# A key stack zeroed by DMA from a row of zeros in DRAM, in place of a GpSimd memset

## The chip, the cores and the metric

The kernel runs on one core of a Trainium2 chip. The metric is the device time of one execution in microseconds (us); lower is better. Engines are named as in the profile: PE is TensorE's matrix multiply and PEld its weight load, DVE is VectorE, ACT is ScalarE, POOL is GpSimd, and SP is SyncE, the engine that issues every DMA of this kernel (its rows in a timeline say SPq).

## What is computed

A block of three stages on x of shape [4, 512, 128] in float32: half a mixture of experts, then an attention, then the same half mixture of experts again.

```python
x = x + 0.5 * ffn(layernorm(x), gate_w, Wg, Wu, Wd)     # 8 experts of 256, each takes its top 128 tokens
x = x + attn(layernorm(x), ...)                         # 16 heads of width 8
x = x + 0.5 * ffn(layernorm(x), gate_w, Wg, Wu, Wd)

def attn(x, Wa, ba, We, be, Wi, Wo, Wv, Wout, ...):
    aperture, expression = sigmoid(x @ Wa + ba), sigmoid(x @ We + be)
    inner, outer, v = x @ Wi, x @ Wo, x @ Wv            # each split in 16 heads of 8
    p = softmax(inner @ outer.T / sqrt(8))
    p = p * aperture[query] * expression[key]
    p = p / (p.sum(-1) + 1e-8)
    heads = rotate(p @ v)                               # a fixed rotation and scale for each head
    return heads @ Wout
```

## The kernel before

All five engines run programs that are written out by hand, with a semaphore for each hand-over; there is no scheduler. The order of the Python text is the order on each engine, and a wait holds everything that stands behind it on its engine.

**The stages.** The first mixture of experts runs until about 136 us of the span, the attention until about 390 us, the second mixture of experts to the end. The experts loop on PE is, for one expert, `gate_up` (12 matmuls, lines 1018 to 1020), `down` (L1035), `turn_down` (transposes, L1042) and `scatter` (L1050 and L1051, which add the expert's rows back to their tokens in four PSUM banks). DVE serves it with `gate_times_up` (L769), `weigh` (L777, L781, L783) and `make_place` (L761, four rows of 0 and 1 that say which token each slot goes to). After the last expert ACT scales the banks, PE turns them (L1079), and DVE adds them to x (`add_moe`, L801), normalizes (`norm_stats` L627 and L630, `norm_apply` L635 and L638), and PE projects (L1100, L1113).

**The key stack.** `k_stack` is [128, 4 groups, 4 heads, 512] in float32, 32 KB in each of 128 partitions, 4.19 MB in all. In the experts its two halves hold the gathered tokens (`picked_hi`, `picked_lo`), which `gate_up` reads. In the attention each half of 64 partitions holds 32 rows of keys for the heads of one parity and a row of ones below them (row 64 jj + 32); all other rows have to be zero, since the products run over all 128 partitions. So between the last `gate_up` of the first mixture of experts and the first load of keys the whole stack is zeroed, and the two rows of ones are written.

**Who clears and who waits.** POOL does it in `attention_constants` (lines 403 to 415), the last thing before it goes to sleep until the attention:

```python
pool.wait_ge(gate_up_done[0], 2 * MI * E)
nc.gpsimd.memset(k_stack[:].bitcast(F32), 0.0).then_inc(pool_consts, 1)
pool.wait_ge(pool_consts, 5)
nc.gpsimd.memset(v_ext[:, :, :, :, DH + 1:DH + 2], 1.0).then_inc(attention_consts, 1)
for jj in range(2):
    ...
    nc.gpsimd.memset(ones_rows.bitcast(F32), 1.0).then_inc(attention_consts, 1)
```

Two engines wait for `attention_consts` to reach 3, that is for the second row of ones: DVE at line 849, ahead of `add_bias(0)` (L835), and SP at line 339. What stands behind SP's wait, in this order: eight DMAs of `clear_max_rows` (L328, rows of zeros into the query stack); `store_parts(0)`, two stores of `part_hi` and two of `part_lo` (L314, 512 KB each, from 128 partitions); a wait for their landing; `load_stacks(0, 0)` (L323, four loads of 128 KB, each into 32 partitions of one half, two for the query stack and then two for the key stack); `store_parts(1)`; the loads of groups 1 to 3. The first products of the attention (`first_maxima`, L1133 on PE, reduced by L807 on DVE) wait for the first group's loads.

Of the kernel before, what the change touches and what calls it, by code (L numbers as in the profile page):

```python
# [12 lines left out]
F32 = mybir.dt.float32  # L13
# [34 lines left out]
def macaron_block(nc, x_in, Wa, ba, We, be, Wi, Wo, Wv, Wout, chi, beta_p, iv_p, ov_p, gate_w, Wg, Wu, Wd, out):  # L48
    B, S, D = x_in.shape
    H = Wa.shape[1]  # L50
    DH = D // H
    E, _, I = Wg.shape
    K = max(1, int(S / E * 2))
    C = S // P
# [3 lines left out]
    MI = I // P  # L58
    G = 4
    HG = H // G  # L60
# [5 lines left out]
    with ExitStack() as ctx:  # L66
        def sb(name, shape, dt=F32):
            return ctx.enter_context(nc.sbuf_tensor(name, shape, dt))

        def sem(name):  # L70
            return ctx.enter_context(nc.semaphore(name))
# [3 lines left out]
        zeros = sb("zeros", [P, S], F16)  # L75
# [68 lines left out]
        k_stack = sb("k_stack", [P, G, HG, S], F32R)  # L144
# [25 lines left out]
        row_i = sb("row_i", [P, 2], I32)  # L170

        parts_dram = nc.dram_tensor("parts_dram", [2, B, H, DH, 4, S], F32, kind="Internal").ap()
        zero_rows_dram = nc.dram_tensor("zero_rows_dram", [PAIRS, S], F32, kind="Internal").ap()

        ps = ctx.enter_context(nc.psum_tensor("ps", [P, 8, 512], F32))
# [3 lines left out]
        pool_consts = sem("pool_consts")  # L179
# [4 lines left out]
        gate_loaded = sem("gate_loaded")  # L184
        attn_weights_loaded = sem("attn_weights_loaded")
        zero_rows_stored = sem("zero_rows_stored")
        out_stored = sem("out_stored")

        def by(n, name):
            return [sem(f"{name}{i}") for i in range(n)]  # L190
# [17 lines left out]
        gate_up_done, silu_ready = by(2, "gate_up_done"), by(2, "silu_ready")  # L208
# [67 lines left out]
        def _(sp):  # L276
# [28 lines left out]
            sp.wait_ge(consts_made, 7)  # L305
            sp.dma_start(zero_rows_dram, zeros[0:PAIRS].bitcast(F32).rearrange("p (a t) -> p a t", a=1).broadcast_to([PAIRS, 2, S // 2])).then_inc(zero_rows_stored, 16)

            def store_parts(b):
                for half, (parts, ready, stored) in enumerate(((part_hi, qk_hi_ready, hi_stored), (part_lo, qk_lo_ready, lo_stored))):
                    for qk in range(2):  # L310
                        blocks = parts_dram[qk, b].rearrange("h d (m n) t -> m n (h d) t", m=2)
                        sp.wait_ge(ready, 2 * b + qk + 1)
                        twice = blocks[half] if qk == 0 else blocks[:, half]
                        sp.dma_start(twice.rearrange("n r t -> r n t"),  # L314
                                     parts[:, b % 2, qk, :].bitcast(F32).unsqueeze(1).broadcast_to([P, 2, S])).then_inc(stored[b % 2][qk], 16)
# [19 lines left out]
                                 max_rows[2 * jj:2 * jj + 2, g % 2, :].bitcast(F32)).then_inc(max_rows_loaded[g], 16)  # L335

            sp.wait_ge(scattered[0], B)
            sp.wait_ge(zero_rows_stored, 16)
            sp.wait_ge(attention_consts, 3)
            for g in range(G):  # L340
                clear_max_rows(g)
            store_parts(0)
            for qk in range(2):
                sp.wait_ge(hi_stored[0][qk], 16)
                sp.wait_ge(lo_stored[0][qk], 16)
            load_stacks(0, 0)
            store_parts(1)
            for g in range(1, G):
                load_stacks(0, g)
            load_max_rows(0, 0)  # L350
            store_parts(2)
            store_parts(3)

# [26 lines left out]
        def _(pool):  # L380
# [22 lines left out]
            def attention_constants():  # L403

                nc.gpsimd.memset(bias_row[:, 0:D], 0.0).then_inc(pool_consts, 1)
                nc.gpsimd.memset(v_ext[:], 0.0).then_inc(pool_consts, 1)
                pool.wait_ge(gate_up_done[0], 2 * MI * E)
                nc.gpsimd.memset(k_stack[:].bitcast(F32), 0.0).then_inc(pool_consts, 1)
                pool.wait_ge(pool_consts, 5)
                nc.gpsimd.memset(v_ext[:, :, :, :, DH + 1:DH + 2], 1.0).then_inc(attention_consts, 1)  # L410

                for jj in range(2):
                    pool.wait_ge(attention_consts, 1 + jj)
                    ones_rows = k_stack[64 * jj + 4 * DH:64 * jj + 4 * DH + 1].rearrange("r g (pp jj) t -> r g jj pp t", jj=2)[:, :, jj]
                    nc.gpsimd.memset(ones_rows.bitcast(F32), 1.0).then_inc(attention_consts, 1)
# [45 lines left out]
            affinity_parts(0)  # L461
            split_weights(0)
            attention_constants()
            pool.wait_ge(attention_consts, 3)
            pool.wait_ge(gates_ready, 2)
# [819 lines left out]
```

## Time and profile before

| | |
|---|---|
| time, median of 3 runs | 518.32 us (517.5 to 518.35) |
| span of the profiled execution, first to last instruction | 516.1 us, so 2.2 us less than the median |
| PE busy | 427.1 us (83%) |
| DVE busy | 400.4 us (78%) |
| ACT busy | 239.9 us (46%) |
| POOL busy | 68.6 us (13%) |
| moved by DMA | 26.03 MB, of it 25.74 MB on the one queue that SP feeds |

Only the span of the profiled execution is known beside the three times; the 2.2 us between it and the median lie before the first and behind the last instruction. A busy share is an average over the whole span. What one edit between two stages is worth is read from the stretch of the timeline around it.

### The profile page before, as it was taken

How to read it: one execution, taken by the hardware profiler on the slowest of the kernel's cores; microseconds unless marked ns; L12 is line 12 of the kernel's file. 1: busy time of each engine (PE TensorE's matmuls, PEld its weight loads, DVE VectorE, ACT ScalarE, POOL GpSimd, SP SyncE). 2: the span in 40 equal slices, each digit the busy share in tenths (PEclk: the TensorE clock that was granted, in tenths of full speed). 3: DMA queues.
4: the chain of work that ended last, by engine and by line, in shares of the span. 5: the costliest groups of instructions: out<-in, count | busy, mean ns of one | idle time of the engine just before them, and what ended most of it. 6: DMA issues, size and time to landing. Idle time of an engine off the chain costs nothing.

```text
span 516.1 us, 7820 instructions
## 1 busy us (share of the span) xinstructions
PE 427.1 (83%) x2252; PEld 250.8 (49%) x2252; DVE 400.4 (78%) x841; ACT 239.9 (46%) x439; POOL 68.6 (13%) x105
## 2 busy tenths in 40 slices
PE   2605999995588899999999999999996506999995
PEld 2501557773454445555555545554553402567773
DVE  6698848899689987778777777777655598768884
ACT  2400443330341267777676777766784201543332
POOL 5510002149000010000000000000002500001100
PEclk9999999998788799999999999999999655999999
DMA  5000012210058810111111111110110000012212
GB/s 166 1 0 1 1 30 62 61 31 0 4 213 276 297 61 25 37 37 43 42 42 42 42 42 42 42 42 1 35 31 0 0 0 2 1 33 59 61 32 81
DMA packets 24749, 26.03 MB, mean 50 GB/s; under 512 B 3634, under 2 KB 16438, under 8 KB 24726
## 3 DMA queue, kind: packets, MB, share of 16 engines
q1 hardware_dynamic: 24726, 25.74, 16.0%
q8 instruction: 12, 0.20, 0.2%
q14 instruction: 11, 0.09, 0.1%
HBM read 16.16 MB, written 9.44 MB: 50 GB/s over the span
## 4 chain that ended last, share of the span: by engine, by line
PE 69%; DVE 25%; issue 3%; ACT 2%; DMA 1%; DVEq 0%; ACTq 0%
PE ps L1133 12%; PE ps L1158 12%; PE ps L1148 10%; DVE neg_max L807 6%; PE ps L999 5%; PE ps L1035 5%; DVE heads_out L707 3%; PE ps L1018 3%; PE ps L1020 3%; PE ps L1019 3%; DVE values L704 3%; PE ps L1050 2%; PE ps L1051 2%; PE ps L960 2%; DVE probs L746 2%
## 5 line engine op out<-in xcount | busy, mean ns | idle before, releaser
L807 DVE TENSOR_REDUCE neg_max<-ps 128x1 f32<-128x512 f32 x256 | 163.4, 684 | 38.9 <-PE ps L1133 38.9
L597 ACT ACTIVATE probs<-ps 128x512 f32<-128x512 f32 x256 | 137.8, 598 | 64.6 <-PE ps L1148 62.9
L1133 PE MATMUL ps<-k_stack,q_stack 128*128 128x512 f32 x256 | 113.7, 452 | 4.8 <-DVE neg_max L807 3.5
L1148 PE MATMUL ps<-q_stack,k_stack 128*128 128x512 f32 x256 | 100.6, 403 | 0.2 <-ACT probs L597 0.2
L1133 PEld LDWEIGHTS ps<-k_stack,q_stack 128*128 128x128 f32 x256 | 49.0, 192 | 68.8 <-DVE neg_max L807 61.7
L1158 PE MATMUL ps<-probs,v_ext 128*32 128x512 f32 x512 | 68.2, 605 | 0.0
L1148 PEld LDWEIGHTS ps<-q_stack,k_stack 128*128 128x128 f32 x256 | 47.7, 190 | 12.7 <-ACT probs L597 5.7
L523 ACT CAST k_stack<-ps 128x512 fp32r<-128x512 f32 x32 | 17.2, 589 | 67.7 <-PE ps L999 67.7
L451 POOL TENSOR_TENSOR w_lo<-w_gu,w_hi 128x512 fp32r<-128x512 f32 x16 | 20.4, 1279 | 149.7 <-ACT w_hi L510 149.7
L769 DVE TENSOR_TENSOR vae_and_gates<-heads_out,ps 128x512 f32<-128x512 f32 x32 | 21.9, 687 | 19.7 <-ACT heads_out L531 17.7
L746 DVE TENSOR_TENSOR probs<-slot_row,slot 128x1024 f16<-128x1024 f16 x32 | 36.5, 1216 | 0.1
L1050 PE MATMUL ps<-q_stack,part_hi 128*128 128x512 f32 x64 | 28.5, 445 | 9.0 <-DVE part_hi L783 9.0
L761 DVE TENSOR_SCALAR q_stack<-token_row,indexT 128x512 fp32r<-128x512 f32 x64 | 33.9, 592 | 0.0
L476 POOL TENSOR_TENSOR v_ext<-vae_and_gates,expression 128x128 f32 (+1 forms) x16 | 6.5, 409 | 205.8 <-PE ps L1158 154.3
L999 PE MATMUL ps<-probs,xn_hi 128*128 128x512 f16 x64 | 26.8, 419 | 7.1 <-DVE probs L746 6.7
L1035 PE MATMUL ps<-vae_and_gates,wd_sb 128*128 128x512 f32 x64 | 30.5, 598 | 0.8 <-DVE vae_and_gates L769 0.8
L1018 PE MATMUL ps<-k_stack,w_hi 128*128 (+1 forms) x64 | 30.3, 474 | 0.8 <-ACT k_stack L523 0.8
L535 ACT COPY down_out<-ps 128x512 f32<-128x512 f32 x16 | 9.4, 588 | 45.4 <-PE ps L1035 45.4
L974 PE MATMUL ps<-ident,threshold_row 32*128 32x32 f32 x2 | 0.6, 309 | 33.4 <-DVE threshold_row L716 33.4
L999 PE MATMUL ps<-probs,xn_lo 128*128 128x512 f16 x64 | 26.9, 420 | 0.0
L1051 PE MATMUL ps<-q_stack,part_hi 128*128 128x512 f32 x64 | 26.9, 420 | 0.0
L531 ACT ACTIVATE heads_out<-ps 128x512 f32<-128x512 f32 x32 | 19.2, 599 | 14.9 <-PE ps L1020 13.1
(151 smaller groups left out, 574.8 us busy)
## 6 DMA issues: line engine op xcount, KB each, us to landing
parts_dram<-part_hi SPq DMA_DIRECT2D x8, 512.0 KB, 3.6
parts_dram<-part_lo SPq DMA_DIRECT2D x8, 512.0 KB, 4.9
q_stack<-parts_dram SPq DMA_DIRECT2D x32, 128.0 KB
k_stack<-parts_dram SPq DMA_DIRECT2D x32, 128.0 KB
w_gu<-in_L_ffn_Wg_dram SPq DMA_DIRECT2D x16, 128.0 KB, 2.1
w_gu<-in_L_ffn_Wu_dram SPq DMA_DIRECT2D x16, 128.0 KB, 2.2
wd_sb<-in_L_ffn_Wd_dram SPq DMA_DIRECT2D x16, 128.0 KB, 2.2
x<-in_L_attn_x_dram SPq DMA_DIRECT2D x4, 256.0 KB, 3.8
```

The source lines that it names most:

```text
L597: nc.scalar.activation(probs[:, u // HG, u % HG, :], ps[:, RING + ring_bank(step, u), :], ACT.Exp, scale=SCORE_SCALE).then_inc(probs_ready, 1)
L746: nc.vector.tensor_tensor(pick[:, b, c], slot_row[:].unsqueeze(1).broadcast_to([P, E, K]), slot[:, c, b * E:(b + 1) * E].unsqueeze(2).broa ...
L761: nc.vector.tensor_scalar(place[:, u, b, :], token_row[:], indexT[:, b, bass.ds(2 * i + o, 1)], None, ALU.is_equal).then_inc(place_ready[l ...
L807: nc.vector.tensor_reduce(neg_max[:, g, qt, col:col + 1], ps[:, ring_bank(step, u), :], AX.X, ALU.max, negate=True).then_inc(max_taken, 1)
L999: last = nc.tensor.matmul(ps[:, pick_bank(n) + k, :], half[:, C * b + c, :], pick[:, b, c, 4 * hf:4 * hf + 4, :], start=(c == 0), stop=(c ...
L1018: nc.tensor.matmul(ps[:, bank, :], w_hi[:, u, k, cols], tokens_hi, start=True, stop=False)
L1035: last = nc.tensor.matmul(ps[:, 6, :], wd_sb[:, u, m, :], hidden[:, u, m, :], start=(m == 0), stop=(m == MI - 1))
L1050: nc.tensor.matmul(ps[:, b, :], wy_hi[:, u, b, :], place[:, u, b, :], start=False, stop=False, skip_group_check=True)
L1051: last = nc.tensor.matmul(ps[:, b, :], wy_lo[:, u, b, :], place[:, u, b, :], start=False, stop=final, skip_group_check=True)
L1133: nc.tensor.matmul(ps[:, ring_bank(step, u), :], q_stack[:, g, pp, chunk(qt)], k_stack[:, g, 2 * pp + jj, :], start=True, stop=True).then_ ...
L1148: nc.tensor.matmul(ps[:, RING + ring_bank(step, u), :], k_stack[:, g, j, chunk(c)], q_stack[:, g, j // 2, :], start=True, stop=True).then_ ...
L1158: last = nc.tensor.matmul(ps[32 * j:32 * j + 32, 6, :], v_ext[:, g, c, j, :], probs[:, c, j, :], start=(c == 0), stop=(c == C - 1))
```

## The change

The memset of the stack on POOL goes. In its place SP writes a row of zeros of 32 KB into DRAM (from the fp16 tile `zeros`, one DMA), waits for it and for the last `gate_up`, and then issues two DMAs of 2.1 MB: each reads that one row 64 times and writes it into one half of 64 partitions of `k_stack`. POOL waits for both before it writes the rows of ones. The two memsets of the rows of ones stay, and so do both waits for `attention_consts`.

```diff
+        zero_stack_dram = nc.dram_tensor("zero_stack_dram", [1, G * HG * S], F32, kind="Internal").ap()
...
+        k_stack_cleared = sem("k_stack_cleared")
...
             sp.dma_start(zero_rows_dram, zeros[0:PAIRS]...).then_inc(zero_rows_stored, 16)
 
+            sp.dma_start(zero_stack_dram.rearrange("a (p t) -> (a p) t", t=S // 2), zeros[0:2 * G * HG].bitcast(F32)).then_inc(zero_rows_stored, 16)
+            sp.wait_ge(zero_rows_stored, 32)
+            sp.wait_ge(gate_up_done[0], 2 * MI * E)
+            for jj in range(2):
+                sp.dma_start(k_stack[64 * jj:64 * jj + 64].bitcast(F32).rearrange("r g j t -> r (g j t)"),
+                             zero_stack_dram.broadcast_to([64, G * HG * S])).then_inc(k_stack_cleared, 16)
...
             sp.wait_ge(scattered[0], B)
-            sp.wait_ge(zero_rows_stored, 16)
             sp.wait_ge(attention_consts, 3)
...
                 nc.gpsimd.memset(v_ext[:], 0.0).then_inc(pool_consts, 1)
-                pool.wait_ge(gate_up_done[0], 2 * MI * E)
-                nc.gpsimd.memset(k_stack[:].bitcast(F32), 0.0).then_inc(pool_consts, 1)
-                pool.wait_ge(pool_consts, 5)
+                pool.wait_ge(pool_consts, 4)
                 nc.gpsimd.memset(v_ext[:, :, :, :, DH + 1:DH + 2], 1.0).then_inc(attention_consts, 1)
 
+                pool.wait_ge(k_stack_cleared, 32)
                 for jj in range(2):
```

On SP, between the last weights of the first experts and the attention's first stores, the kernel before has these rows (what is written, what is read, the shape):

```order
L306 DMA zero_rows_dram<-zeros 4x1x256 [waits consts_made]
L328 DMA q_stack<-zero_rows_dram 1x1024 [waits attention_consts,zero_rows_stored,scattered0]
L328 DMA q_stack<-zero_rows_dram 1x1024 x7
L314 DMA parts_dram<-part_hi 128x2x512 [waits qk_hi_ready]
```

The changed kernel has these at the same place:

```order
L308 DMA zero_rows_dram<-zeros 4x1x256 [waits consts_made]
L310 DMA zero_stack_dram<-zeros 32x256
L314 DMA k_stack<-zero_stack_dram 64x8192 [waits gate_up_done0,zero_rows_stored]
L314 DMA k_stack<-zero_stack_dram 64x8192
L337 DMA q_stack<-zero_rows_dram 1x1024 [waits attention_consts,scattered0]
L337 DMA q_stack<-zero_rows_dram 1x1024 x7
L323 DMA parts_dram<-part_hi 128x2x512 [waits qk_hi_ready]
```

Three DMAs came in ahead of `clear_max_rows`, and nothing else moved on SP. On POOL, behind the last expert's weights, the kernel before has:

```order
L405 MEMSET bias_row 128x128
L406 MEMSET v_ext 128x2048
L408 MEMSET k_stack 128x8192 [waits gate_up_done0]
L410 MEMSET v_ext 128x64 [waits pool_consts]
L415 MEMSET k_stack 1x8x512 [waits attention_consts] x2
```

The changed kernel has there:

```order
L413 MEMSET bias_row 128x128
L414 MEMSET v_ext 128x2048
L416 MEMSET v_ext 128x64 [waits pool_consts]
L422 MEMSET k_stack 1x8x512 [waits attention_consts,k_stack_cleared]
L422 MEMSET k_stack 1x8x512 [waits attention_consts]
```

One memset left, and the first row of ones took on a wait for the two DMAs. The order on the other engines is the same.

## Rows read from the trace of the kernel before

**Rows 1.** The page: busy time of two engines, and the last chain by engine.

```profile
PE 427.1 (83%) x2252; PEld 250.8 (49%) x2252; DVE 400.4 (78%) x841; ACT 239.9 (46%) x439; POOL 68.6 (13%) x105
PE 69%; DVE 25%; issue 3%; ACT 2%; DMA 1%; DVEq 0%; ACTq 0%
```

**Rows 2.** Timeline of POOL: start us, us, engine, line, operation, count, idle before.

```profile
114.69 6.93 POOL L408 MEMSET k_stack<- 128x8192 f32 x1 [2.00 <-PE ps L1020]
121.68 0.37 POOL L410 MEMSET v_ext<- 128x64 f32 x1
122.10 7.24 POOL L415 MEMSET k_stack<- 1x4096 f32 x2
```

**Rows 3.** Timeline of DVE in the same stretch.

```profile
116.02 5.88 DVE L781 CAST part_hi<-weighted 128x512 fp32r<-128x512 f32 x1
121.94 0.69 DVE L783 TENSOR_TENSOR part_hi<-weighted,part_hi 128x512 fp32r<-128x512 f32 x1
122.54 7.86 DVE L761 TENSOR_SCALAR q_stack<-token_row,indexT 128x512 fp32r<-128x512 f32 x4
...
131.04 0.43 DVE L781 CAST part_hi<-weighted 128x512 fp32r<-128x512 f32 x1
```

**Rows 4.** Timeline of PE, the end of the first mixture of experts.

```profile
116.76 1.88 PE L1035 MATMUL ps<-vae_and_gates,wd_sb 128*128 128x512 f32 x4
...
132.34 0.77 PE L1050 MATMUL ps<-q_stack,part_hi 128*128 128x512 f32 x1 [5.95 <-DVE part_hi L783]
...
135.89 2.14 PE L1079 MATMUL ps<-ident,combined 128*128 128x128 f32 x16
```

**Rows 5.** Timeline of PE, the end of the second mixture of experts.

```profile
502.13 1.88 PE L1035 MATMUL ps<-vae_and_gates,wd_sb 128*128 128x512 f32 x4
...
509.32 1.91 PE L1079 MATMUL ps<-ident,combined 128*128 128x128 f32 x16
```

**Rows 6.** Waits of SP: who was waited for, us, times, longest.

```profile
SPq L339 <- POOL k_stack L415: 21.8, 1, 21.8
```

**Rows 7.** Timeline of SP: DMA issues, start us and us.

```profile
136.13 2.31 SPq L328 DMA_DIRECT2D q_stack<-zero_rows_dram  x8
143.42 1.51 SPq L314 DMA_DIRECT2D parts_dram<-part_hi  x2
147.21 1.17 SPq L314 DMA_DIRECT2D parts_dram<-part_lo  x2
151.48 0.84 SPq L323 DMA_DIRECT2D q_stack<-parts_dram  x2
...
190.94 0.89 SPq L323 DMA_DIRECT2D q_stack<-parts_dram  x2
```

**Rows 8.** Windows, all engines; last two columns: DMA share and GB/s.

```profile
144.30:144.60 0.30, 0.00 (x0) 0.00 (x0) 0.27 (x4) 0.00 (x0) 0.00 (x0) 1.00 0.90 341
147.50:148.00 0.50, 0.50 (x4) 0.50 (x4) 0.50 (x3) 0.24 (x1) 0.00 (x0) 0.50 0.00 0
150.80:151.20 0.40, 0.40 (x2) 0.02 (x1) 0.40 (x2) 0.37 (x1) 0.00 (x0) 1.00 0.25 87
160.00:166.00 6.00, 4.86 (x9) 1.75 (x9) 6.00 (x11) 0.00 (x0) 0.00 (x0) 0.81 0.91 262
172.00:181.00 9.00, 7.70 (x25) 4.13 (x23) 8.93 (x16) 2.39 (x5) 0.11 (x1) 0.81 1.03 379
192.40:192.80 0.40, 0.40 (x2) 0.32 (x3) 0.00 (x0) 0.11 (x1) 0.00 (x0) 1.00 0.85 200
192.80:194.00 1.20, 1.20 (x9) 0.93 (x7) 0.91 (x2) 0.60 (x1) 0.00 (x0) 1.00 0.77 273
```

**Rows 9.** Timeline of DVE at the start of the attention.

```profile
139.47 1.11 DVE L638 TENSOR_SCALAR xn<-x,mean_var,rstd 128x128 f32<-128x128 f32 x4
...
150.58 0.88 DVE L835 TENSOR_TENSOR vae_and_gates<-ps,bias_row 128x320 f32<-128x320 f32 x2
...
156.75 9.65 DVE L807 TENSOR_REDUCE neg_max<-ps 128x1 f32<-128x512 f32 x16
```

## The prediction

> **What bounds the kernel now.** I read the page first: PE is busy 83% of the span, DVE 78%, and the chain that ended last is 69% PE and 25% DVE [rows 1]. POOL and DMA carry almost none of it. So an edit on POOL and on the DMA queue can only count through what they hold up, and that is read in the timeline of the 40 us in which the stack is cleared.
>
> POOL's timeline comes next. Its memset of the stack starts at 114.69, when the last `gate_up` is done, and takes 6.93 us; the two rows of ones end at 129.34, and with that `attention_consts` is complete [rows 2]. The reader is to see in DVE's timeline what this does beside it. The cast L781 takes 5.88 us from 116.02, until POOL's memset is over, and 0.43 us at 131.04, when POOL is idle; four L761 take 7.86 us beside the rows of ones [rows 3]. DVE stands still while POOL's memset runs. PE waits for it: the last scatter starts at 132.34 after 5.95 us of idle time, and the turning L1079 at 135.89, which is 19.1 us after the last `down` at 116.76 [rows 4]. The second mixture of experts runs the same instructions with no memset beside them, and there it is 7.2 us, from 502.13 to 509.32 [rows 5]. So the memsets cost the end of the first stage 11.9 us.
>
> What the constants are waited for comes last. They were ready at 129.34, SP's 21.8 us behind them [rows 6] ended there, and the next thing that SP needed, the last scatter, came at 136.13 [rows 7]. Before, the clear and its rows of ones were 6.8 us early for SP and, with L835 at 150.58, 21 us early for DVE [rows 9].
>
> **What the change does, part by part.**
>
> Removed: 6.93 us of memset on POOL, and with it the stall of L781. If nothing else bound, L1079 would start at 116.8 + 7.2 = 124.0 instead of 135.9, for the two rows of ones then no longer fall on L761. That is the prize, 11.9 us.
>
> Added, at no cost: the 32 KB row of zeros is written at about 107.6, behind L306, while SP has nothing to do until 114.7; POOL's 0.37 us memset of `v_ext` runs earlier.
>
> Added, with a price: the constants now come later. Step by step, with r for the rate of the two clears in GB/s and 4194 KB to write:
> - issue at 114.7, since SP waits for the same semaphore as POOL did [rows 2];
> - 0.9 us to the first data, as from the issue at 143.42 to 144.3 [rows 7, 8];
> - 4194/r;
> - 0.6 us from the last data, about 150.9, to the reader's release at 151.48 [rows 7, 8];
> - 7.3 us for the two rows of ones and their waits [rows 2].
>
> So the constants are ready at 123.5 + 4194/r. Behind that, on SP, which is the engine with most queued behind the wait: 2.3 us for the eight DMAs of `clear_max_rows`; then the four stores of `store_parts(0)`. Their data are long ready by then, for the first stage ended earlier. Before, they took from 143.42 to 151.48, 8.1 us, of which about 1.0 us was a gap (no data from 147.1 to 148.1, a wait for `part_lo`) [rows 7, 8]; without it 7.1 us. So the first loads are issued 9.4 us after the constants. They are ready 3.5 us later: in the attention's loop four like them are issued from 190.94 and their data end at 194.0, plus 0.6 us less 0.2 us for a slower issue there [rows 7, 8]. Another 0.5 us for the first product, and DVE starts L807 at 136.9 + 4194/r. Before it started at 156.75 [rows 9]. What lies behind is the same work in the same order, paced by DVE. The net is
>
> 4194/r − 19.9 us, with break-even at r = 211 GB/s.
>
> DVE's own wait at line 849 costs nothing beside this: L835 to L807 was 6.2 us before [rows 9], against 13.4 us on SP's path.
>
> **The rate** is what the trace does not show: nothing in it writes 64 partitions with 32 KB each, or reads one row of DRAM 64 times. The rows nearest to it are the loads of the stacks, each into 32 partitions of one half: 262 GB/s while 160 to 166 us hold nothing else, 273 and 200 GB/s in two pieces of the loop's loads. The stores from 128 partitions ran at 379 GB/s [rows 8]. So a narrower destination is slower here. By 379 the clears take 11.1 us, by 262 16.0 us, by 200 21.0 us. I take the middle of 200 and 262, about 230 GB/s: the small loads change the half every 128 or 256 KB, the clears stay for 2.1 MB in one, so I go below their mean, but not below their slowest piece. 4194/230 = 18.2 us: the last clear lands at 134.4, the constants are ready at 141.7, SP issues the first loads at 151.1 and DVE starts L807 at 155.1. The net is −1.6 us: 11.9 us of stall taken away, 10.3 us of them given back to a later clear. Against the span of 516.1 us that is 514.5 us, and with the 2.2 us around it 516.7 us, 1.6 us below the median of 518.32 us. Its own range, for 262 to 200 GB/s, is −3.9 to +1.1 us, 514.4 to 519.4 us.
>
> **A cap on the gain.** However fast the clear, the rows of ones move with it, and they stop DVE's L638 as they stopped L761. Without stalls L638 would first run at 139.47 − 11.9 = 127.6. At 379 GB/s the clear has landed at 127.3 and the rows of ones fill 127.3 to 134.6, so the first L638 group ends about 135 in place of 140.6. The gain is then 5.6 us, not the 8.8 us of the formula. At 300 GB/s (rows of ones from 130.2 to 137.5) the second group is caught, and the gain is about 5 us.
>
> **The rivals.**
>
> *Full rate.* The clears run at 300 to 379 GB/s, for the source is one 32 KB row and each piece is long. For it: the 128-partition stores, 379 GB/s [rows 8]. Against it: no load into a part of the partitions came near it. It gives −5.0 to −5.6 us by the cap, 512.7 to 513.3 us.
>
> *Half rate.* A transfer into one half of the partitions gets half of what the full width gets, 379/2 = 190 GB/s, and the second clear queues behind the first. 4194/190 = 22.1 us, so +2.2 us: 520.5 us. For it: the narrow loads are all below the wide stores. Against it: 262 GB/s over 6 us is 1.4 times 190, though those loads alternate between the halves. The Trainium skill (SBUF — State Buffer, Door 1: The DMA port swizzle) states this as a rule: partitions 0 to 63 reach 8 of 16 ports, 196 GB/s at 1 MiB and 218 in the limit, and two transfers on the two halves gain only 6%. By its 218 the sum would be 19.2 us and −0.6 us, by its 196 21.4 us and +1.5 us. No run here has shown it for a transfer of this size.
>
> *One hot row (slower).* All DMA engines read the same 32 KB of DRAM at the same time, and the rate falls below 190 GB/s because of it. Its place is the wait of POOL's first row of ones for the clears; it decides for slower from 200 GB/s down (+1.0 us), at 150 GB/s it is +8.1 us (526.4 us), at 170 +4.8 us. For it: no row shows such a read of any size. Against it: nothing. The Trainium skill (DMA: Bandwidth & Descriptors, Latency and other measured facts) has copies between HBM tensors with a large power of two between rows fall from 207 to 103 GB/s; by 103 the clears would take 40.7 us, and the sum would be +20.8 us. No row here bears on it.
>
> *No effect.* The DVE stall is not POOL's doing, and the clear is early anyway. The pair 5.88 and 0.43 us for one instruction [rows 3] speaks against it: 518.3 us.
>
> **How the numbers follow.** The forecast (200 to 262 GB/s) 0.45; full rate, with what lies between 262 and 300, 0.17; half rate 0.18; one hot row 0.17; no effect 0.03. About 0.2% (1.04 us) is what a measurement of this kernel can tell from no change: faster from 222 GB/s up, slower from 200 down. Of the forecast's 0.45, 0.28 lie above 222, 0.15 between and 0.02 at the slow end. Faster: 0.28 + 0.17 = 0.45. Same: 0.15 + 0.04 of half rate + 0.03 = 0.22. Slower: 0.02 + 0.14 + 0.17 = 0.33. The range reaches from the cap, 512.7 us, to 524.4 us, which is 162 GB/s: it leaves out what lies below 162 GB/s, somewhat over 0.1, and a few in a hundred below the cap.
>
> **What the changed profile would show.** L781 at about 116 takes 0.43 us, four L761 1.7 us, and L1079 starts near 124. Both clears are issued near 114.8; the DMA windows behind give the rate, and the first row of ones starts near 134.4. L638 between 134 and 142 is drawn out to the end of the rows of ones. SP's longest wait in this stretch is still for the rows of ones, now to about 141.7, and `clear_max_rows` follows at once. PE is idle for several us before the first L1133, near 154.6, where before it went from L1113 to L1133 without a pause. Behind that both traces run alike, shifted by one amount. Wrong would be: a rate outside 200 to 262 GB/s; stores or loads that take longer than 7.1 and 3.5 us once they are back to back; or a second clear that overlaps the first at full width.

## The result and the profile after

The changed kernel takes 524.52 us (median of 4 runs, 522.56 to 525.46) beside 518.34 us for the kernel before (4 runs). The ratio is 1.0115, with a 95% interval of 1.0091 to 1.0138: slower by some 6 us, where a gain of 1.6 us was forecast. The line numbers of the changed kernel are higher: L781 is now L788, L761 L768, L638 L645, L807 L814, L1035 L1042, L1079 L1086, L1100 L1107, L1133 L1140, L339 L347. In the runs further below they shift by a few lines again, and the view names the tiles.

The page after: busy times and the last chain by engine, which answer to [rows 1].

```profile
PE 431.8 (83%) x2252; PEld 254.3 (49%) x2252; DVE 395.4 (76%) x841; ACT 239.4 (46%) x439; POOL 61.7 (12%) x104
PE 74%; DVE 19%; issue 3%; ACT 2%; DMA 1%; DVEq 0%; ACTq 0%
```

POOL lost its 6.9 us and DVE 5 us of busy time, and the kernel is slower. The timelines show why. First those of DVE and of PE at the end of the first mixture of experts:

```profile
116.63 0.43 DVE L788 CAST part_hi<-weighted 128x512 fp32r<-128x512 f32 x1
...
117.70 1.67 DVE L768 TENSOR_SCALAR q_stack<-token_row,indexT 128x512 fp32r<-128x512 f32 x4
```

```profile
116.77 1.88 PE L1042 MATMUL ps<-vae_and_gates,wd_sb 128*128 128x512 f32 x4
...
123.97 1.91 PE L1086 MATMUL ps<-ident,combined 128*128 128x128 f32 x16
```

The cast that took 5.88 us takes 0.43 us, the four L761 that took 7.86 us take 1.67 us, and the turning starts at 123.97 in place of 135.89 [rows 3, 4]. So the prize of 11.9 us was there and was won. The timelines of SP and POOL, the time to landing of the two clears, and SP's wait show what came after it:

```profile
114.73 1.16 SPq L314 DMA_DIRECT2D k_stack<-zero_stack_dram  x2
144.63 2.26 SPq L337 DMA_DIRECT2D q_stack<-zero_rows_dram  x8
146.93 1.09 SPq L323 DMA_DIRECT2D parts_dram<-part_hi  x2
148.07 1.99 SPq L323 DMA_DIRECT2D parts_dram<-part_lo  x2
153.95 0.83 SPq L332 DMA_DIRECT2D q_stack<-parts_dram  x2
```

```profile
137.45 7.10 POOL L422 MEMSET k_stack<- 1x4096 f32 x2 [24.81 <-DMA k_stack<-zero_stack_dram]
```

```profile
DMA to landing us min/median/max: 12.2/17.2/22.1
```

```profile
SPq L347 <- POOL k_stack L422: 28.7, 1, 28.7
```

The first clear (issued at 114.7) lands 12.2 us later, at 126.9, the second (issued at 115.3) after 22.1 us, at 137.4. Between the two landings lie 10.5 us for 2097 KB, which is 200 GB/s. POOL starts the rows of ones at once, they end at 144.55, SP goes on at 144.63, and the first loads are issued at 153.95, where before it was 151.48 [rows 7]. The start of the attention on DVE and on PE:

```profile
138.32 6.38 DVE L645 TENSOR_SCALAR xn<-x,mean_var,rstd 128x128 f32<-128x128 f32 x4
...
158.70 1.89 DVE L814 TENSOR_REDUCE neg_max<-ps 128x1 f32<-128x512 f32 x3 [3.25 <-PE ps L1140]
163.40 7.87 DVE L814 TENSOR_REDUCE neg_max<-ps 128x1 f32<-128x512 f32 x13 [2.81 <-PE ps L1140]
```

```profile
157.90 1.62 PE L1140 MATMUL ps<-k_stack,q_stack 128*128 128x512 f32 x3 [5.69 <-issue]
159.32 1.91 PE L1107 MATMUL ps<-xnT,wi_sb 128*128 128x512 f32 x2
161.02 1.91 PE L1107 MATMUL ps<-xnT,wo_sb 128*128 128x512 f32 x2
161.94 8.38 PE L1140 MATMUL ps<-k_stack,q_stack 128*128 128x512 f32 x13
```

The reader is to see two pauses of DVE here. The first one, 3.25 us, is the wait for the first loads. The second one, 2.81 us, stands between the third and the fourth reduction: PE does the last query and key projection there (L1107), at 1.91 us for each pair of matmuls that takes 1.02 us at full clock (at 136.67 of the same trace). The granted clock was 0.50 from 157.9 to 163.0, the lower of the two levels, after PE had idled for 5.69 us. The kernel before has the same projection at the same place, at full clock:

```profile
155.51 0.97 PE L1133 MATMUL ps<-k_stack,q_stack 128*128 128x512 f32 x3
156.32 1.02 PE L1100 MATMUL ps<-xnT,wi_sb 128*128 128x512 f32 x2
157.18 1.02 PE L1100 MATMUL ps<-xnT,wo_sb 128*128 128x512 f32 x2
157.63 7.82 PE L1133 MATMUL ps<-k_stack,q_stack 128*128 128x512 f32 x13
```

There DVE started at 156.75 and ran 16 reductions without a pause [rows 9], so its fourth began at about 158.6. Now the fourth starts at 163.40, 4.8 us later.

### The profile page after: what moved, and what is told of

It is laid out like the page before. It is cut to its first block, busy times and chain, and to the rows that moved or that the text cites. A ratio compares the mean times of both kernels' runs of the same rounds, so it can differ in the third digit from the quotient of the medians.

```text
span 523.2 us, 7824 instructions
## 1 busy us (share of the span) xinstructions
PE 431.8 (83%) x2252; PEld 254.3 (49%) x2252; DVE 395.4 (76%) x841; ACT 239.4 (46%) x439; POOL 61.7 (12%) x104
## 4 chain that ended last, share of the span: by engine, by line
PE 74%; DVE 19%; issue 3%; ACT 2%; DMA 1%; DVEq 0%; ACTq 0%
PE ps L1140 13%; PE ps L1165 12%; PE ps L1155 10%; PE ps L1042 5%; PE ps L1006 5%; DVE neg_max L814 4%; PE ps L1025 3%; PE ps L1027 3%; PE ps L1026 3%; DVE heads_out L714 3%; DVE values L711 3%; PE ps L1057 3%; PE ps L1058 2%; PE ps L967 2%; PE ps L1107 2%
## 5 line engine op out<-in xcount | busy, mean ns | idle before, releaser
L814 DVE TENSOR_REDUCE neg_max<-ps 128x1 f32<-128x512 f32 x256 | 163.6, 685 | 44.9 <-PE ps L1140 44.9
L1140 PE MATMUL ps<-k_stack,q_stack 128*128 128x512 f32 x256 | 114.9, 461 | 10.8 <-issue 5.7
L1140 PEld LDWEIGHTS ps<-k_stack,q_stack 128*128 128x128 f32 x256 | 49.9, 196 | 75.4 <-DVE neg_max L814 61.5
L1042 PE MATMUL ps<-vae_and_gates,wd_sb 128*128 128x512 f32 x64 | 30.5, 598 | 0.8 <-DVE vae_and_gates L776 0.8
L1057 PE MATMUL ps<-q_stack,part_hi 128*128 128x512 f32 x64 | 26.5, 414 | 0.4 <-DVE part_hi L790 0.4
L768 DVE TENSOR_SCALAR q_stack<-token_row,indexT 128x512 fp32r<-128x512 f32 x64 | 26.7, 481 | 0.0
L1027 PE MATMUL ps<-k_stack,w_lo 128*128 (+1 forms) x64 | 25.2, 394 | 0.0
```

The costliest lines, as they stand in the source:

```text
L768: nc.vector.tensor_scalar(place[:, u, b, :], token_row[:], indexT[:, b, bass.ds(2 * i + o, 1)], None, ALU.is_equal).then_inc(place_ready[l ...
L814: nc.vector.tensor_reduce(neg_max[:, g, qt, col:col + 1], ps[:, ring_bank(step, u), :], AX.X, ALU.max, negate=True).then_inc(max_taken, 1)
L1027: nc.tensor.matmul(ps[:, bank, :], w_lo[:, u, k, cols], tokens_hi, start=False, stop=True).then_inc(gate_up_done[l], 1)
L1042: last = nc.tensor.matmul(ps[:, 6, :], wd_sb[:, u, m, :], hidden[:, u, m, :], start=(m == 0), stop=(m == MI - 1))
L1057: nc.tensor.matmul(ps[:, b, :], wy_hi[:, u, b, :], place[:, u, b, :], start=False, stop=False, skip_group_check=True)
L1140: nc.tensor.matmul(ps[:, ring_bank(step, u), :], q_stack[:, g, pp, chunk(qt)], k_stack[:, g, 2 * pp + jj, :], start=True, stop=True).then_ ...
```

## The experiments

Four runs ask what sets the rate of the clears, three what stands behind it. All were timed beside the kernel before on the same chip (its median was 518.94 us beside the first four and 518.01 us beside the last three); ratios are against it.

**One clear at full width, from one row.**

```diff
-            for jj in range(2):
-                sp.dma_start(k_stack[64 * jj:64 * jj + 64]...,
-                             zero_stack_dram.broadcast_to([64, G * HG * S])).then_inc(k_stack_cleared, 16)
+            sp.dma_start(k_stack[:]..., zero_stack_dram.broadcast_to([P, G * HG * S])).then_inc(k_stack_cleared, 16)
```

> The changed kernel, but the stack is cleared by one DMA into all 128 partitions, still from the one row of 32 KB in DRAM. Theory A (a transfer into 64 partitions gets half of the full width's rate): the clear runs at about 380 GB/s, lands about 12.5 us after its issue in place of 22.7 us, the rows of ones start near 127.5, and the time is near 513 us (the cap of about 5.5 us below before). Theory B (one hot row in DRAM sets the 200 GB/s): the clear still takes 21 us or more and the time stays near 524 us.

515.25 us, ratio 0.9911 (0.9874 to 0.9948). Time to landing of the clear, and the timelines of POOL and DVE:

```profile
DMA to landing us min/median/max: 12.0/12.0/12.0
```

```profile
127.11 7.10 POOL L421 MEMSET k_stack<- 1x4096 f32 x2 [13.42 <-DMA k_stack<-zero_stack_dram]
```

```profile
127.68 6.69 DVE L644 TENSOR_SCALAR xn<-x,mean_var,rstd 128x128 f32<-128x128 f32 x4
...
151.85 9.64 DVE L813 TENSOR_REDUCE neg_max<-ps 128x1 f32<-128x512 f32 x16
```

The same 4.19 MB from the same row land after 12.0 us, not 22.7 us after the first issue. Less the 1.5 us of latency that the prediction used (0.9 and 0.6 us), that is 10.5 us, 400 GB/s. One hot row is no limit even at twice the rate. The rows of ones now fall on the first group of normalizations (L638 before, L644 here), as the cap said, and DVE starts 4.9 us earlier than before.

**Two clears into the halves, from rows of their own.** The row of zeros becomes an image of 128 rows.

```diff
-        zero_stack_dram = nc.dram_tensor("zero_stack_dram", [1, G * HG * S], F32, kind="Internal").ap()
+        zero_stack_dram = nc.dram_tensor("zero_stack_dram", [P, G * HG * S], F32, kind="Internal").ap()
...
+            sp.dma_start(zero_stack_dram.rearrange("p (a t) -> p a t", t=S // 2),
+                         zeros[:].bitcast(F32).unsqueeze(1).broadcast_to([P, 2 * G * HG, S // 2])).then_inc(zero_rows_stored, 16)
...
-                             zero_stack_dram.broadcast_to([64, G * HG * S])).then_inc(k_stack_cleared, 16)
+                             zero_stack_dram[64 * jj:64 * jj + 64]).then_inc(k_stack_cleared, 16)
```

> The changed kernel, its two clears into 64 partitions each kept, but they read 128 rows of 32 KB of their own (4.19 MB of zeros, stored in DRAM from about 12 us on, far ahead). Theory A: nothing changes, the second clear lands 21 to 23 us after the first issue, 524 us. Theory B: the clears run at 300 to 380 GB/s and the time is near 513 us.

523.75 us, ratio 1.0085 (1.0057 to 1.0114). Time to landing:

```profile
DMA to landing us min/median/max: 12.8/17.7/22.5
```

With rows of their own the halves are no faster, so the hot row is ruled out from this side too.

**One clear at full width, from rows of its own.** The image, and the one DMA of the first run.

> Both at once: one DMA into 128 partitions, from 128 rows of its own. Theories A and B both expect about 380 GB/s and 513 us; if it is faster than the run with one row at full width, the hot row costs something at the higher rate. If it stays at 200 GB/s, both fall, and the size of the pieces (32 KB) is the next suspect.

513.21 us, ratio 0.9889 (0.9857 to 0.9920). Time to landing, and DVE:

```profile
DMA to landing us min/median/max: 12.3/12.3/12.3
```

```profile
151.85 9.65 DVE L816 TENSOR_REDUCE neg_max<-ps 128x1 f32<-128x512 f32 x16
```

The landing takes 12.3 us against 12.0, and the first reduction (L807 before) starts at 151.85 in both: whether the source is one row or 128 makes no difference here. The medians lie 2 us apart, but the intervals of the two ratios overlap.

**The halves in turn.** 16 DMAs of 256 KB, from one row, the half changed after each. POOL waits for all 16.

```diff
+            for piece in range(8):
+                at = slice(1024 * piece, 1024 * piece + 1024)
                 for jj in range(2):
-                    ...
+                    sp.dma_start(k_stack[64 * jj:64 * jj + 64]...[:, at],
+                                 zero_stack_dram[:, at].broadcast_to([64, 1024])).then_inc(k_stack_cleared, 16)
```

> The changed kernel with its two clears cut into 16 of 256 KB that go to the two halves in turn (4 KB in each of 64 partitions), from the same one row. The reason that the prediction gave for a rate between 200 and 262 GB/s was that small loads change the half and so overlap. If that holds, about 260 GB/s, the last clear lands about 17.5 us after the first issue, and the time is 518 to 520 us. If two halves in turn do not overlap, 200 GB/s and 524 us.

522.69 us, ratio 1.0071 (1.0047 to 1.0094). The issues, the time to landing, and POOL:

```profile
L316 SPq DMA_DIRECT2D k_stack<-zero_stack_dram x16: 513/597/602, 115.6 to 125.1; - x16
```

```profile
DMA to landing us min/median/max: 3.5/7.7/11.5
```

```profile
136.69 7.10 POOL L424 MEMSET k_stack<- 1x4096 f32 x2 [22.64 <-DMA k_stack<-zero_stack_dram]
```

From the first issue at 115.6 to POOL's start it is 21.1 us; less 1.5 us that is 19.6 us and 214 GB/s. Changing the half gives 7% over the two large clears, not the 30% that the reason for my rate needed. All pieces were issued by 125.7, some 11 us before POOL's start, so SP's issue is not what held them.

**The projection ahead of the first products.**

```diff
-            first_maxima(0, range(RING))
             project_qk(3)
+            first_maxima(0, range(RING))
```

> The changed kernel, but PE runs project_qk(3) before the first three products of first_maxima(0) in place of behind them, in the 5 us in which it waits for the first loads anyway. Theory: 2.8 us of the loss come from this projection, which a PE at half clock (1.91 us for each of its two products) puts between the third and the fourth product while VectorE has nothing else left. Then VectorE's 2.8 us of idle time behind its third reduction go, L814 runs through, and the time falls by 2.8 us, to near 521.7 us. Rival: the pause is the loads' or the throttle's own, and the time stays at 524.5 us.

520.21 us, ratio 1.0060 (1.0041 to 1.0080), against 1.0115 (1.0091 to 1.0138) without the edit; the intervals do not touch. Timelines of PE and DVE:

```profile
153.10 1.10 PE L1107 MATMUL ps<-xnT,wi_sb 128*128 128x512 f32 x2 [2.08 <-DVE part_lo L835]
154.35 1.56 PE L1107 MATMUL ps<-xnT,wo_sb 128*128 128x512 f32 x2 [0.16 <-DVE part_lo L835]
...
157.52 9.54 PE L1140 MATMUL ps<-k_stack,q_stack 128*128 128x512 f32 x16 [1.60 <-DMA k_stack<-parts_dram]
```

```profile
158.35 9.66 DVE L814 TENSOR_REDUCE neg_max<-ps 128x1 f32<-128x512 f32 x16 [3.26 <-PE ps L1140]
```

The pause of 2.81 us is gone and 16 reductions run through. By the ratios the edit is worth 2.8 us (1.0115 − 1.0060 = 0.0055 of 518 us), and the two intervals leave some 1.5 us either way. PE's wait before its first product is now put down to the DMA of the key stack: the loads are what is late.

**The ones written by DMA too.** The image of 128 rows holds the ones in its rows 32 and 96, stored there early in the first stage from a small tile `ones_f32`. With that, one DMA at full width brings zeros and ones, POOL has no memset of the stack left, and SP waits for the clear itself.

```diff
+            for jj in range(2):
+                sp.dma_start(zero_stack_dram[64 * jj + 4 * DH].rearrange("(n jj t) -> jj n t", jj=2, t=S)[jj],
+                             ones_f32[0:8]).then_inc(zero_rows_stored, 16)
...
-            sp.wait_ge(attention_consts, 3)
+            sp.wait_ge(attention_consts, 1)
+            sp.wait_ge(k_stack_cleared, 16)
...
-                for jj in range(2):
-                    pool.wait_ge(attention_consts, 1 + jj)
-                    ones_rows = ...
-                    nc.gpsimd.memset(ones_rows.bitcast(F32), 1.0).then_inc(attention_consts, 1)
```

> The clear at full width from 128 rows of DRAM of its own, of which the rows 32 and 96 already hold the ones (written there from a small tile of ones from 25 us on), so that no memset is left on POOL in this stretch and SyncE waits for the clear itself. Theory (what is left of the cost at full rate are the two rows of ones, which stop VectorE's L638): the whole 11.9 us come out. The turning starts near 124.0, the clear lands near 127.2 and the first store can still go out in time, L807 starts at about 145, and the time is 506 to 507.5 us. Rival: SyncE, now held until 127.2 in place of 124.2, or the first loads, set the start, and 2 to 3 us of it stay lost: 509 us.

506.74 us, ratio 0.9780 (0.9766 to 0.9795): by the ratio 11.4 us faster than before, and the fastest version here. PE, SP and DVE:

```profile
124.89 1.91 PE L1092 MATMUL ps<-ident,combined 128*128 128x128 f32 x16
```

```profile
127.91 2.31 SPq L345 DMA_DIRECT2D q_stack<-zero_rows_dram  x8
```

```profile
128.23 1.11 DVE L651 TENSOR_SCALAR xn<-x,mean_var,rstd 128x128 f32<-128x128 f32 x4
...
146.38 9.66 DVE L820 TENSOR_REDUCE neg_max<-ps 128x1 f32<-128x512 f32 x16
```

DVE starts its first reduction 10.4 us earlier than before. That is 1.4 us later than expected. Of these, 0.9 us are there already at the turning (124.89 for 123.97) and also at SP's weight loads in the first stage (85.89 for 84.97 in the changed kernel), long before the clear; what causes them is not shown. From the run with one clear from its own rows to this one the first reduction comes 5.5 us earlier (151.85 to 146.38), and by the ratios (0.9889 and 0.9780) the time falls by 5.6 us: that is the price of the two rows of ones on POOL.

**The same with the projection first.**

> The run with ones by DMA and with project_qk(3) first. Theory: where the loads are not late the projection was hidden behind VectorE, so putting it first costs the first products its 1.0 to 2.0 us: 0 to +2 us against the run with ones by DMA alone. Rival: it gains here too, by up to 2.8 us.

508.25 us, ratio 0.9821 (0.9802 to 0.9841), by the ratios 2.1 us above the run without it. DVE:

```profile
146.86 9.66 DVE L820 TENSOR_REDUCE neg_max<-ps 128x1 f32<-128x512 f32 x16 [0.93 <-PE ps L1146]
```

Where the loads are in time, the projection was hidden behind DVE. Put first, it makes DVE wait 0.93 us, and from the turning to the first reduction it is 22.5 us (124.37 to 146.86) where it was 21.5 us. The medians say that the edit costs, but the two traces bear out only this 1.0 us, and it does not last in them: the third group of reductions starts 39.4 us after the turning here and 39.3 us after it without the edit. So the same two lines that gained 2.8 us when the loads were late gain nothing when they are in time; how much they cost there stays open.

## Why the prediction was wrong

**Right:** the stall and its size. L781 and L761 fell to 0.43 and 1.67 us and the turning came at 123.97, where 124.0 was forecast. Right too was the path that it is given back on: clear, rows of ones, SP's queue. From the constants (144.55) to the first loads (153.95) it is 9.4 us, as worked out. The cap held: at full rate the start gained 4.9 us where 5.6 was forecast, and the times, 515.25 and 513.21 us, lie near its 512.7 us.

**Wrong, the rate.** "I take the middle of 200 and 262, about 230 GB/s" was the term that was mis-sized. It measured 200 GB/s, the low end. The constants came at 144.55 in place of 141.7, 2.9 us of the loss. With break-even at 211 GB/s this alone turns the sign. It does not give the size: for 200 GB/s the prediction's own sum is +1.1 us, 519.4 us, and the measured loss is some 6 us. The reason that I gave, that small loads change the half and so overlap, was put to the test with pieces of 256 KB, and they gained 7%. Why the loads of the stacks showed 262 GB/s, with pieces of 128 KB in 32 partitions, is open. The rival of half rate had the mechanism right: 200 GB/s into 64 partitions, 400 GB/s into 128, and the one DRAM row takes no part. The Trainium skill (SBUF — State Buffer, Door 1: The DMA port swizzle) has partitions 0 to 63 reach 8 of 16 ports, with 196 GB/s at 1 MiB and about 218 in the limit; the trace agrees, with 200 GB/s at 2 MB. The Trainium skill (SBUF — State Buffer, "Can I just issue two DMAs to hit both halves?") has two DMAs on the two halves gain only 6% over one; the run with the halves in turn agrees, with 7%. I had given this rival 0.18 and rated above it a window in which narrow loads alternate.

**Wrong, the pace behind it.** "What lies behind is the same work in the same order, paced by DVE" failed at "paced by DVE", and with it the forecast that both traces run alike from there, shifted by one amount; the term was put at nothing. Before, DVE came to its first reduction 1.2 us behind PE's first product (156.75 and 155.51), for it still had biases to add, and the projection that PE puts between its third and fourth product went unseen. In the changed kernel DVE had finished everything else and waited for the loads. So the projection, at the lower clock (granted 0.50), showed as a pause of 2.81 us. Both other runs with late clears and this order have it too (2.18 us with own rows, 2.00 us with the halves in turn), and the run with the projection first gives it back. The half-rate rival's time, 520.5 us, lies close to the 520.21 us of that run and not to the 524.52 us of the change, for the rival did not have this pause either. That it comes so close is in part luck: its 190 GB/s is below the 200 measured, and this makes up for the small terms that it leaves out.

**Small terms.** The first product came 3.95 us after the loads' issue where 3.5 were taken, and it took 0.8 us to DVE's start at the reduced clock where 0.5 were taken: 0.8 us. Together: −1.6 + 2.9 + 0.8 + 2.8 is +4.9 us, and the fourth reduction shows 4.8 (163.40 against 158.6). SP's weights for the second mixture of experts come 5.1 us later, and the profiled execution then loses 1.6 us more. The issues before and after, at the end of the attention and in the experts, first of the kernel before and then of the changed one:

```profile
371.46 0.40 SPq L282 DMA_DIRECT2D w_gu<-in_L_ffn_Wg_dram  x1
...
457.82 0.34 SPq L282 DMA_DIRECT2D w_gu<-in_L_ffn_Wg_dram  x1
```

```profile
376.56 0.72 SPq L284 DMA_DIRECT2D w_gu<-in_L_ffn_Wg_dram  x1
...
464.53 0.34 SPq L284 DMA_DIRECT2D w_gu<-in_L_ffn_Wg_dram  x1
```

That stretch is 86.4 us before and 88.0 us after. VectorE is busy for the same 59.2 us in both, but PE for 61.6 us in place of 58.2, and the granted clock is 0.75 in place of 0.80. In the run with halves from their own rows, which starts the attention just as late, the stretch is 86.1 us (375.56 to 461.70) at a clock of 0.80. So the 1.6 us go with a lower clock in this one execution and do not follow from the delay. The four timed runs show the same: those with a mean granted clock of 0.931 took 524.88 and 525.46 us, the one with 0.942, about the clock of the profiled run before (0.943), took 522.56 us. So part of the 6.2 us between the medians goes with the clock; how much of it the change itself brings about stays open.

## What to carry to other kernels

A wait that is early by 7 us on one queue is no reason to call its work free or its replacement cheap: work out the new landing time and compare it with the first reader, after the stall that you remove has moved that reader forward. A large DMA into half of the partitions is costed at half the rate, and a long clear wants all 128 in one transfer. When a memset on GpSimd stops VectorE, take all such memsets out of the stretch, since here the two rows of one partition each cost as much as the clear of the whole stack; and look in the other engine's order for work that was only hidden because the reader came late.

## What the runs showed of the hardware

- Two DMAs into 64 partitions each wrote 200 GB/s and followed each other; one DMA of the same bytes in all into 128 partitions wrote 400 GB/s. 16 pieces in turn reached 214 GB/s.
- Reading one 32 KB row of DRAM 128 times went as fast as reading 128 rows once (12.0 and 12.3 us to landing).
- A GpSimd memset of one partition held VectorE up like one of 128: four tensor_scalar that take 1.11 us together took 6.69 us beside the two rows of ones (7.10 us), as the cast of 0.43 us took 5.88 us beside the memset of 128 partitions (6.93 us).
- PE's granted clock was 0.50 after an idle time of 5.69 us, and a pair of 128x512 matmuls took 1.91 us in place of 1.02.
